# Two attention blocks on one core: tiles regrouped by heads, convolution taps shared out over three engines, horizontal offsets as differences, and minus the maximum in a row of q

## What is computed

```python
x = x + block0(_gn(x), ...)      # w_qkv, pooling taps, layer norms, rel_pos, w_proj
x = x + block1(_gn(x), ...)      # qkv_w with a low-rank addition to q and v, rel_pos, proj_w

# block0, for 12 heads of 16 channels
q, k, v = split(x @ w_qkv.T + b_qkv)
q = layer_norm(dwconv3x3(q, w_pool_q), g_q, b_q)      # likewise k and v, own taps, gains and biases
attn = einsum(q * scale, k) + rel_h[..., :, None] + rel_w[..., None, :]
o = softmax(attn) @ v + q                              # q is added again (ori_q)
y = o @ w_proj.T + b_proj
```

## Time and profile before

| what | us |
|---|---|
| median of 3 runs | 109.63 (109.55 to 111.31) |
| the profiled execution | 108.68 |
| its span, first to last instruction | 106.7 |

### The profile page before, as it was taken

One profiled execution on the slowest core, in us unless ns is written; L12 is line 12 of the kernel. 1 busy time (PEld: TensorE's weight loads), 2 busy tenths in 40 slices (PEclk: granted clock), 3 DMA queues, 4 the chain that ended last, 5 costly groups with the idle time before them and its releaser, 6 DMA issues.

```text
span 106.7 us, 2097 instructions
## 1 busy us (share of the span) xinstructions
PE 97.1 (91%) x822; PEld 70.8 (66%) x825; DVE 62.7 (59%) x134; ACT 51.3 (48%) x115; POOL 31.4 (29%) x46
## 2 busy tenths in 40 slices
PE   5799999999959999999999999899989999999780
PEld 2155787578848986777856563797759879857440
DVE  3469995587999667834650135464796493560130
ACT  4011904663534981837815624254246668715820
POOL 8947600599999999000000000000000000000000
PEclk9995579999999999999999999999999999999999
DMA  2999980000000000000000000000000000000002
GB/s 59 308 307 292 237 79 0 3 0 6 0 0 0 9 0 0 0 0 6 0 0 0 0 6 0 0 0 0 0 0 6 0 0 6 0 0 0 0 0 74
DMA packets 2826, 3.73 MB, mean 35 GB/s; under 512 B 305, under 2 KB 2242, under 8 KB 2818
## 3 DMA queue, kind: packets, MB, share of 16 engines
q0 software_dynamic: 784, 0.79, 6.7%
q1 hardware_dynamic: 1282, 1.41, 4.8%
q10 hardware_dynamic: 752, 1.42, 4.5%
HBM read 3.42 MB, written 0.20 MB: 34 GB/s over the span
## 4 chain that ended last, share of the span: by engine, by line
PE 75%; DVE 10%; ACT 7%; DMA 3%; issue 2%
PE bank L917 9%; PE bank L760 8%; PE bank L853 6%; PE bank L850 6%; PE bank L749 6%; PE bank L892 5%; PE bank L905 5%; PE bank L866 5%; PE bank L893 4%; PE bank L831 3%; ACT pt L386 3%; DVE taps_m L622 3%; DMA x<-x_t 3%; PE bank L734 3%; PE bank L832 2%
## 5 line engine op out<-in xcount | busy, mean ns | idle before, releaser
L575 DVE TENSOR_REDUCE mx<-bank 128x2 fp32r<-128x512 f32 x24 | 15.0, 682 | 3.2 <-PE bank L866 3.2
L386 ACT ACTIVATE pt<-bank 128x512 f32<-128x512 f32 x24 | 13.0, 594 | 3.6 <-PE bank L893 3.4
L892 PE MATMUL bank<-qs,ks 128*128 128x256 f32 x48 | 13.3, 310 | 0.8 <-ACT pt L386 0.7
L570 DVE SCALAR_TENSOR_TENSOR qs<-qs,vec,bank 64x512 fp32r<-64x512 f32 x12 | 8.8, 737 | 6.9 <-ACT qs L376 6.8
L893 PE MATMUL bank<-mt,nhot_r 128*128 128x256 f32 x48 | 12.0, 280 | 0.0
L892 PEld LDWEIGHTS bank<-qs,ks 128*128 128x128 f32 x48 | 9.0, 187 | 2.8 <-ACT pt L386 1.8
L760 PE MATMUL bank<-pad,taps_m 128*128 128x256 f32 x36 | 10.5, 445 | 0.2 <-DVE taps_m L622 0.2
L734 PE MATMUL bank<-warm 128*128 128x512 bf16 x28 | 9.0, 443 | 1.5 <-POOL warm L279 1.3
L324 POOL TENSOR_SCALAR tap_p<-pad,vec 64x256 f32<-64x256 f32 (+1 forms) x11 | 10.3, 937 | 0.0
L749 PE MATMUL bank<-xn,w 96*128 96x256 f32 (+1 forms) x40 | 9.6, 428 | 0.6 <-DVE xn L549 0.6
L376 ACT ACTIVATE qs<-bank 64x512 fp32r<-64x512 f32 x12 | 7.1, 590 | 6.2 <-PE bank L853 6.2
(11 more groups left out here) (103 smaller groups left out, 166.7 us busy)
## 6 DMA issues: line engine op xcount, KB each, us to landing
ks<-hots POOLq DMA_DIRECT2D x1, 768.0 KB, 7.8
wp<-w_proj ACTq DMA_DIRECT2D x1, 576.0 KB, 8.1
w<-w_qkv SPq DMA_DIRECT2D x1, 432.0 KB, 8.8
w<-w_qkv SPq DMA_DIRECT2D x1, 288.0 KB, 4.8
cst<-consts ACTq DMA_DIRECT2D x1, 256.0 KB, 4.8
nhot<-neg_hot ACTq DMA_DIRECT2D x1, 256.0 KB, 5.7
x<-x_t SPq DMA_DIRECT2D x1, 192.0 KB, 3.3
wpq<-w_proj_q ACTq DMA_DIRECT2D x1, 192.0 KB, 8.9
```

Of the source, the lines that this page charges most:

```text
L386: act.activation(pt[:, h, :, :], key_banks[h % 2][:, :].rearrange("p (k n) -> p k n", k=QT), ACT.Exp).then_inc(exped[b], 1)
L575: dve.tensor_reduce(mx[:, h, :], ring_bank(h // 4, 4 + h % 4)[:, :].rearrange("p (q n) -> p q n", q=QT), AXX, ALU.max).then_inc(maxed[b], 1)
L892: pe.matmul(dst, ks[:, h, k * 128:(k + 1) * 128], qs[:, h, :], start=True, stop=False)
```

## The change

- The q and k of one head group now share a tile: T0, T1, T2 hold q and k of heads 0 to 3, 4 to 7, 8 to 11 (weights' columns are reordered on the host); C and E hold v as before. A stage needs only its own tile. Both blocks use it; `late_k` goes.
- The taps are shared out: T0 three on PE and six on DVE, T1 five and four, C five on DVE and four on GpSimd, T2 six and three, E nine on GpSimd. Five tap matrices instead of eighteen are made, as T0 and T1 have the same taps: three by DVE, two by ACT. A centring pass adds the summed taps onto PE's.
- `normalise` multiplies gain and reciprocal deviation in one operation; the bias comes in ACT's high part, DVE's low part, `value` (DVE, for C and E) and `residual` (ACT, q rows for `q_project`).
- GpSimd makes the horizontal offsets as differences from the first key column's offset (`differences`), so that row 0 of `qs` is zero and free. `ks` row 0 is one everywhere (in `hots`, now laid out for 12 heads on the host), and minus the maximum is written into row 0 of `qs`: `turn_maxima` makes it as rows of one partition by eight matmuls with one column of weights (identity times -1), ACT copies two heads, DVE two. The matmuls with `nhot_r`, `nhot`'s transfer and `mt` go.
- x comes in two halves, on SP's and ACT's queues; warm-ups ahead of the group sums and behind them are 8 and 5 instead of 7 and 4, `lora_first` comes later, and two warm-ups in block 0's stage 1 go.
- `lora_second(0)` and `add_lora(0)` move from stage 1 to stage 2 of block 0, `q_project(0)` behind that stage.

```diff
+PE_TAPS = {T0: range(0, 3), T1: range(0, 5), C: (), T2: (), E: ()}
+DVE_TAPS = {T0: range(3, 9), T1: range(5, 9), C: range(0, 5), T2: range(0, 6)}
+POOL_TAPS = {C: range(5, 9), T2: range(6, 9), E: range(0, 9)}
+MATRICES = 5
...
-    sp.dma_start(xs[0][0:HALF], x_t.rearrange("(t p) n -> p t n", p=HALF)).then_inc(d_x, 16)
+    sp.dma_start(xs[0][0:HALF, 0], x_t[0:HALF]).then_inc(d_x[0], 16)
...
+    pool.wait_ge(d_rel, 16)
+    pool.wait_ge(d_vec, 16)
+    pool.wait_ge(rel_zeroed, 1)
+    def differences(b):
+        row = relt[64:128, 2 * b + 1, 0:1]
+        src = bass.AP(row.tensor, row.offset, [list(row.ap[0]), [1, SIDE], [1, SIDE]])
+        first = bass.AP(row.tensor, row.offset, [list(row.ap[0]), [1, SIDE], [0, SIDE]])
+        pool.tensor_tensor(dif[64:128, b], src, first, ALU.subtract).then_inc(dif_set, 1)
+        pool.wait_ge(dif_set, b + 1)
+        pool.tensor_copy(dif_hi[64:128, b], dif[64:128, b]).then_inc(dif_high, 1)
+        pool.wait_ge(dif_high, b + 1)
+        pool.tensor_scalar(dif_m[64:128, b], dif_hi[64:128, b].bitcast(F32), vec[64:128, MASK:MASK + 1], None,
+                           ALU.mult).then_inc(dif_masked, 1)
+        pool.wait_ge(dif_masked, b + 1)
+        for c in (0, 16):
+            pool.tensor_tensor(rel_w[64:128, 2 * b + 1, :, c:c + 16], dif_m[64:128, b], dif[64:128, b],
+                               ALU.add).then_inc(rel_set, 1)
+            pool.wait_ge(rel_set, 4 * b + c // 16 + 1)
+    def windows(b):
+        row = relt_s[64:128, 2 * b, 0:1]
+        src = bass.AP(row.tensor, row.offset, [list(row.ap[0]), [1, SIDE], [1, SIDE]])
+        for c in (32, 48):
+            pool.tensor_copy(rel_w[64:128, 2 * b, :, c:c + 16], src).then_inc(rel_set, 1)
+    differences(0)
     pool.wait_ge(rel_split, 1)
...
-    pool.wait_ge(p_sum, 2 * TAPS - D_SPLIT)
+    convolve_pool(C)
+    convolve_pool(T2)
+    pool.wait_ge(p_sum, pool_sums(T2))
+    pool.wait_ge(d_cst, 16)
+    ident_four = bass.AP(ident.tensor, ident.offset, [[ident.ap[0][0], HALF], [0, 4], [1, HALF]])
+    pool.tensor_copy(add_w[0:HALF].rearrange("p b t n -> p (b t) n"),
+                     ident_four).then_inc(add_set, 1)
+    pool.wait_ge(add_set, 1)
+    convolve_pool(E)
+    pool.wait_ge(p_sum, pool_sums(E))
+    differences(1)
...
+    act.dma_start(xs[0][0:HALF, 1], x_t[HALF:]).then_inc(d_x[1], 16)
...
-        if b == 0 and g == 0:
-            act.wait_ge(mt_zeroed, 1)
-        act.activation(mt[0:4, g, :], mt_ps, ACT.Copy).then_inc(max_c[b], 1)
+        act.wait_ge(max_t[b], 2 * g + 1)
+        act.activation(qs[0:1, 4 * g:4 * g + 2, :], mt_ps[0].rearrange("p (h n) -> p h n", h=2),
+                       ACT.Copy).then_inc(max_a[b], 1)
...
+        act.wait_ge(scaled, n_cen[t])
+        act.activation(hi[:, t, :], nrm[:, t, :], ACT.Identity,
+                       bias=vec[:, LNB0 + t:LNB0 + t + 1]).then_inc(hi_set[0], 1)
+    def residual(t):
+        to = qf[0:64, 0] if t == T0 else qf[64:128, 0] if t == T1 else qf[0:64, 1]
+        act.wait_ge(scaled, n_cen[t])
+        act.activation(to, nrm[0:64, t, :], ACT.Identity, bias=vec[0:64, LNB0 + t:LNB0 + t + 1]).then_inc(qf_set, 1)
...
     act.wait_ge(zeroed, 1)
-    pad_tile(0)
-    pad_tile(1)
+    pad_tile(T0)
+    pad_tile(C)
+    pad_tile(T1)
+    set_picks()
+    tile_stats(T0)
+    tap_matrices(PE_TAPS[T0].stop)
+    tile_rstd(T0)
+    pad_tile(T2)
+    high(T0)
     copy_lora()
...
-    tile_stats(B)
-    pad_tile(4)
-    high(A)
-    tile_rstd(B)
-    stage(0, 0, {0: lambda: high(B), 1: lambda: tile_stats(C), 2: lambda: tile_rstd(C), 3: lambda: tile_stats(D)})
-    stage(0, 1, {0: lambda: tile_rstd(D), 1: lambda: high(D)})
+    def k_stats():
+        tile_rstd(T1)
+    def after_first():
+        high(T1)
+        residual(T0)
+        pad_tile(E)
+    def c_in():
+        tile_stats(C)
+        tile_rstd(C)
+    stage(0, 0, {0: lambda: tile_stats(T1), 4: k_stats, 1: after_first, 3: c_in})
+    stage(0, 1, {0: lambda: residual(T1), 1: lambda: tile_stats(T2), 2: lambda: tile_rstd(T2), 3: lambda: high(T2)})
     stage(0, 2, {1: stats_e, 2: lambda: tile_rstd(E), 3: v_to_tokens_e})
+    residual(T2)
     last_stage(0)
...
+        dve.scalar_tensor_tensor(out=nrm[0:r, t, :], in0=cen_e[:] if t == E else cen_ps[t][0:r],
+                                 scalar=vec[0:r, LNG0 + t:LNG0 + t + 1], in1=rstd[0:r, t, :],
+                                 op0=ALU.mult, op1=ALU.mult).then_inc(scaled, 1)
+    def value(t):
+        r = ROWS[t]
+        dve.wait_ge(scaled, n_cen[t])
+        dve.tensor_scalar(full[0:r, (C, E).index(t), :], nrm[0:r, t, :], vec[0:r, LNB0 + t:LNB0 + t + 1], None,
+                          ALU.add).then_inc(full_set, 1)
...
+    def copy_maxima(b, g):
+        dve.wait_ge(max_t[b], 2 * g + 2)
+        dve.tensor_copy(qs[0:1, 4 * g + 2:4 * g + 4, :],
+                        mt_ps[1].rearrange("p (h n) -> p h n", h=2)).then_inc(max_d[b], 1)
...
+    taps(T0, 0, 6)
...
         dve.tensor_copy(va[:, :, 0:8, 0:HD],
                         turn_ps[:, 0:QT * HD * 8].rearrange("p (q h c) -> p q h c", q=QT, c=HD)).then_inc(v_set[0], 1)
-    def low_d_and_v():
-        low(D)
+    def t1_norm():
+        normalise(T1)
+    def t1_low():
+        low(T1)
+        taps(C, 3, 5)
+    def c_norm():
+        normalise(C)
+        value(C)
+    def t2_in():
         v_to_tokens()
-        add_lora(0)
-    stage(0, 0, {0: k_in, 2: lambda: taps(D, 2, 4), 3: lambda: taps(D, 4, D_SPLIT)})
-    normalise(C)
-    stage(0, 1, {1: lambda: normalise(D), 2: low_d_and_v})
-    stage(0, 2, {1: lambda: add_lora(1), 2: lambda: normalise(E)})
+        low(T2)
+    stage(0, 0, {1: lambda: taps(C, 1, 3), 4: t1_norm, 2: t1_low})
+    taps(T2, 0, 3)
+    c_norm()
+    stage(0, 1, {0: lambda: taps(T2, 3, 5), 1: lambda: taps(T2, 5, 6), 2: lambda: normalise(T2), 3: t2_in})
+    add_lora(0)
+    stage(0, 2, {1: lambda: add_lora(1), 2: lambda: (normalise(E), value(E))})
+    copy_maxima(0, HG - 1)
     o_norm(0, HG - 2)
     o_norm(0, HG - 1)
...
+    def convolve(t, first, last):
+        for k in PE_TAPS[t][first:last]:
+            if k == 0:
+                pe.wait_ge(padded, n_padded[t])
+            if t == T0:
+                pe.wait_ge(taps_d, k + 1)
+            if t == T1 and k == PE_TAPS[T0].stop:
+                pe.wait_ge(taps_a, MATRICES - PE_TAPS[T0].stop)
+            pe.matmul(cen_ps[t], taps_m[:, k, :], pad[:, t, k // 3:k // 3 + SIDE, k % 3:k % 3 + SIDE],
+                      start=(k == 0), stop=False, skip_group_check=True)
...
+    def centre_tile(t):
         r = ROWS[t]
-        if first == 0:
-            pe.wait_ge(qtaps_set if v == 0 else vtaps_set, TAPS)
-            pe.wait_ge(padded, order0.index(t) + 1)
-        for k in range(first, last):
-            mm = pe.matmul(cen_ps[t][0:r, :], taps_m[:, v, k, 0:r],
-                           pad[:, t, k // 3:k // 3 + SIDE, k % 3:k % 3 + SIDE],
-                           start=(k == 0), stop=(k == TAPS - 1))
-            if k == TAPS - 1:
-                mm.then_inc(centred, 1)
+        parts = []
+        if t in DVE_TAPS:
+            pe.wait_ge(conv_step[t], len(DVE_TAPS[t]))
+            parts.append(conv[0:r, conv_slot[t], :])
+        if t in POOL_TAPS:
+            pe.wait_ge(p_sum, pool_sums(t))
+            parts.append(conv_p[0:r, pool_order.index(t), :])
+        if t == T2:
+            pe.wait_ge(lora_c, 1)
+        if t == E:
...
-            dst = ring_bank(g, n)[:, j * TOK:(j + 1) * TOK]
-            pe.matmul(dst, pick[:, v, i:i + 2, :], hi[:, place3[t], :], start=True, stop=False)
-            mm = pe.matmul(dst, pick[:, v + 1, i:i + 2, :], lo[:, place3[t], :], start=False, stop=True)
+        for part, ready in enumerate((hi_set, lo_set)):
+            pe.wait_ge(ready[b], g + 1)
+            for j in range(2):
+                t, i = place(4 * g + 2 * j)
+                mm = pe.matmul(ring_bank(g, n)[:, j * TOK:(j + 1) * TOK], pick[:, v + part, i:i + 2, :],
+                               (hi, lo)[part][:, t, :], start=(part == 0 and j == 0), stop=(part == 1), skip_group_check=True)
...
         if g >= 1:
-            pe.wait_ge(exped[b], 4 * g - 1)
-        for q in range(QT):
-            mm = pe.matmul(mt_ps[:, q * 128:(q + 1) * 128], mx[:, 4 * g:4 * g + 4, q], ident_r[:],
-                           start=True, stop=True)
-        mm.then_inc(max_t[b], 1)
+            pe.wait_ge(exped[b], 4 * g)
+        for j in range(4):
+            for q in range(QT):
+                to = (j % 2) * TOK + q * 128
+                mm = pe.matmul(mt_ps[j // 2][:, to:to + 128], mx[:, 4 * g + j, q:q + 1], ident_r[:],
...
+                mm.then_inc(max_t[b], 1)
     def score_by_key(b, h):
         g, j = h // 4, h % 4
         if j == 0:
-            pe.wait_ge(max_c[b], g + 1)
-        if b == 0 and h == 1:
-            pe.wait_ge(logged, n_cen[D])
+            pe.wait_ge(max_a[b], g + 1)
+        if j == 1:
+            pe.wait_ge(max_d[b], g + 1)
         if h >= 2:
```

(37 more changed lines are left out.)

397 lines of the change are left out of this document (180 added, 217 removed).

## The result

The changed kernel took 116.17 us (median; 114.71 to 117.59) beside 109.59 us (109.41 to 111.31) for the kernel before on the same chip: a ratio of 1.0478, 95% interval 1.0447 to 1.0508. It is slower by 4.8%, where 108.3 us, a gain of 1.2%, was forecast; the range ended at 111.3. Its profiled execution took 114.81 us, the span of it 113.0 us, against 106.7 before.

The account below looks back on a forecast made before the run. PE work, busy 91%, was taken as the bound, with a DVE queue behind block 0's first scores. Block 0's 0.6 us and block 1's 0.7 made 1.3 us: 108.68 to 107.4 profiled, 108.3 median; range 105.5 to 111.3.

Parts of the forecast that it names:

- block 1's further 0.7: Block 1's gain of 0.7 us up to its direct sums, on top of block 0's 0.6.
- The 48 matmuls: Adding minus the maximum: 5.8 us of PE time, but only about 0.5 us a stage, 0.6 to 0.7 in a last stage.
- The head: Kernel start: 0.3 us from x in halves, T0 centred at 14.7 to 14.9, first pick at 18.7.
- the clock comes back sooner, or does not fall: Rival: the head's low clock from 8.0 ends early or never comes; 106.2 us taken, chance 0.25.
- the windows: Two GpSimd operations in the head, 0.9 us, following the differences; done at 13.5, wanted at 20.6, off the path.
- The turning: Maxima turned by eight one-column matmuls: 0.48 us, bounds 0.27 and 0.96, so +0.36 a stage.
- The copies: Copies of the turned maxima, one row of 512: ACT 0.37 to 0.59 us, DVE 0.41 to 0.69, upper ends taken.
- the gap: Block 0's stage 1: PE waits for DVE from 28.7 to 32.3, with only 0.5 us to do.
- the clock falls in the gap of stage 1: Rival: half clock in block 0 from the gap to 38 adds 3.0 us, giving 111.3; chance 0.20.
- the slower case: The rival "the clock falls in the gap of stage 1": 111.3 us, slower by 1.5%, chance 0.20.

Follow-up runs that it names:

- experiment 5: Changed kernel plus twelve zero matmuls in block 0's stage 1 gap and 512-column zero matmuls in PE's waits for exponentials: 111.69 us, ratio 1.0264.
- experiment 8: experiment 5 with the residual of T2 moved early on ScalarE, to the start of block 0's stage 2: 110.75 us.
- experiment 10: experiment 8 with the q projection put back in block 0's stage 2: 110.11 us.
- experiment 19: experiment 13 measured again in five rounds: 108.14 us, ratio 0.9841.
- experiment 9: Changed kernel with the maxima as before (two turning matmuls, 48 one-hot matmuls), so the tiles alone: 116.49 us, ratio 1.0703.
- experiment 6: Changed kernel with a zero matmul ahead of each of the 48 key-score matmuls and twelve in block 0's stage 1: 115.19 us.
- experiment 3: Kernel before without only the 48 matmuls that add minus the maximum: 115.44 us, beside 108.13 for the kernel before.
- experiment 12: Changed kernel with the maxima as before, twelve zero matmuls in stage 1's gap, residual of T2 early, q projection back in stage 2: 117.47 us.
- experiment 13: experiment 10 with lora_second(0) moved from stage 2's picks into PE's wait ahead of the first weighing: 106.75 us, ratio 0.9765.
- experiment 2: Changed kernel with twelve 256-column zero matmuls in block 0's stage 1, between the second pick and the turning: 112.33 us.
- experiment 1: Changed kernel with a 256-column zero matmul ahead of each of the 48 key-score matmuls: 117.73 us.
- experiment 11: Kernel before with 8 and 5 warm-ups in its head and x in two halves: 110.63 us, ratio 0.9988.
- experiment 14: experiment 7 measured again in more runs: 108.91 us, ratio 0.9896.
- experiment 20: Changed kernel with only lora_second(0), T2's residual and the q projection moved, no zero matmuls: 109.37 us, ratio 1.001.
- experiment 7: Kernel before with 8 and 5 warm-ups in its head instead of 7 and 4: 107.17 us, ratio 0.9861.

## Why the prediction was wrong

**The sum of the work was priced well, in part by luck.** Without its low time the changed kernel's S0 is 40.6 - 13.7 x 0.43 = 34.7 us; the forecast had 59.6 - 24.7 = 34.9. S1 is 41.8 - 6.8 x 0.43 = 38.9; the forecast, with block 1's further 0.7, had 38.9 too, and experiments 5, 8, 10 and 19 show 38.9 to 39.0 with no low clock at all. In S0 the agreement hides two misses: a wait of 1.0 us that the forecast overlooked (below), and 1.2 us by which the rest came out cheaper. The 48 matmuls are worth 0.6 to 0.7 us in block 1, as forecast (39.6 with them or with zero matmuls in their place and no low clock, experiments 9 and 6, 38.9 to 39.0 without), and not the 2.9 that half of 5.8 us of PE time seems to promise.

**The head was better than forecast.** T0's centring matmul ran at 12.86, not 14.7 to 14.9: the clock didn't fall at 8 (rival "the clock comes back sooner, or does not fall"), PE waited for DVE's taps, as that rival said. Two of those taps took 0.84 us each (at 11.11 and 11.98), beside GpSimd's two-tensor additions, where 0.58 a step was taken. Pick at 17.49 (18.7), scores at 24.05 (24.7), stage 1's relative unit at 30.77 (32.3).

GpSimd in order of time, where the differences meet DVE's taps:

```profile
8.58 0.61 POOL L306 TENSOR_TENSOR dif<-relt 64x256 f32<-64x256 f32 x1
9.25 0.39 POOL L308 CAST dif_hi<-dif 64x256 fp32r<-64x256 f32 x1
9.75 0.98 POOL L310 TENSOR_SCALAR dif_m<-dif_hi,vec 64x256 f32<-64x256 f32 x1
10.81 1.71 POOL L314 TENSOR_TENSOR rel_w<-dif_m,dif 64x256 fp32r<-64x256 f32 x2
13.58 1.06 POOL L323 CAST rel_w<-relt_s 64x256 fp32r<-64x256 f32 x2 [1.05 <-DVE relt_s L702]
```

The differences ended at 12.52 and the windows at 14.64, a microsecond later than the 13.5 forecast, since the windows waited 1.05 for DVE's split of the table; wanted at 19.59, they are on no path. The Trainium skill (GPSIMD Engine Reference, Specifications) names DVE operations with two SBUF inputs as those that contend; the trace agrees, and the price depends on what GpSimd runs: 0.60 (at 9.96) beside its one-tensor mask, 0.84 beside its two-tensor additions.

**The small new operations.** The turning took 0.48 for eight, as taken, between its bounds of 0.27 and 0.96. The copies are at their upper ends (groups by form, columns as in the earlier trace rows):

```profile
L637 DVE CAST qs<-bank 1x512 fp32r<-1x512 f32 x6 | 4.1, 677 | 7.7 <-PE bank L948 7.6
L408 ACT ACTIVATE qs<-bank 1x512 fp32r<-1x512 f32 x6 | 3.5, 584 | 4.0 <-PE bank L948 3.9
```

DVE was the releaser of PE's wait in the gap, 1.50 us ahead of the turning, as forecast.

**The step that failed is the clock behind the first scores.** The forecast put it at full level there in both blocks, so the low clock was a term of nothing in its sum, and only the rival "the clock falls in the gap of stage 1" gave it a price: one fall, +3.0 us, with a chance of 0.20. Measured were four falls, two in each block, 20.5 us low and some 8.8 us of time. The rival's mechanism ran: the clock fell at 32.5, behind the gap, with +3.0 forecast for it and 7.0 us low x 0.43 = 3.0 measured. Against it stood that the old kernel idled 1.2 of 3.8 us and kept the clock. That argument took the busy share of a stretch for what the clock follows. It isn't: 2.67 of 3.40 busy was followed by a fall here, 2.62 of 3.80 before wasn't, and 3.35 of 3.40 was followed by one at 87.25. What the prediction never asked is what else the 48 matmuls did. They are the dense part of each output side (128 rows by 128 columns, 256 wide), and between them stand relative units, turnings and low-rank matmuls, small and many. Experiment 3 takes only them from the old kernel and loses 4.1 us by the fastest runs, 7.3 by the medians; experiments 5 and 9 put dense work back in two ways and block 1 has no fall, while in experiment 12 it has one.

The second term missed is the move of `lora_second(0)` beside stage 2's picks, the new turning and a relative unit. It was priced as 0.82 us of PE time. Between experiments 10 and 13 its place is the only difference, and in the profiled executions stage 2's fall went with it: 6.8 us low in the changed kernel and 10.2 in experiment 10, 2.9 to 4.4 us of time. It is not the only way to that fall: in experiment 3 it stands in stage 1 and stage 2 falls all the same. The Trainium skill (TensorE: Matmul & The Clock Gate, The HAM clock gate) has the throttled state as the default that activity has to release. That sentence stood in the prediction as speaking for the slower case, and the runs side with it over the single row that stood against it. It gives no reason for the falls behind 3.35 and 3.40 of 3.40 us busy.

**The sum.** Forecast span 106.7 - 1.3 = 105.4. Add 8.8 for the low clock; take off 0.65 for the head up to the scores, 0.2 for S0's working and 0.4 for the tail (6.6 us behind block 1's direct sums against 6.95): 112.95, of 113.0 measured. The price of 0.43 is known to some 0.02, so this sum holds to half a microsecond at best. Of S0, 1.0 us is a wait that the forecast overlooked: `q_project(0)`, moved behind stage 2, waits for ScalarE's residual of T2, which was queued behind the output copy.

One row of PE in order of time:

```profile
58.30 1.03 PE L987 MATMUL bank<-qf,wpq 128*96 128x256 f32 x3 [1.00 <-ACT qf L500]
```

**What stays open.** Which property of a stretch of matmuls the clock follows: columns of weights, rows, width or distance all differ at once between the dense and the thin ones. No run separates them. It is open, too, why the clock of the same kernel falls behind the gap of stage 1 in one execution (19) and not in another (13); the head differed by 0.3 us. And the fall in experiment 2, behind 3.40 of 3.40 us busy, is tied by experiment 13 to what stands in that place, since without `lora_second(0)` it went; whether its matmuls of 16 rows hold the clock less, or only their 0.8 us at that moment, isn't shown.

## What to carry to other kernels

Before you take matmuls out of a kernel, ask what they do for the clock: dense matmuls between small ones can cost little and hold it up, and where other engines pace the stage anyway, taking them away gains little (0.7 us a block here) and may cost several times that. Look at the clock line first after a change and price each low microsecond (0.43 us here); a busy share near 90% is no protection. Put small, unhurried matmuls into PE's waits rather than beside other small ones. Where times vary between executions of one kernel, compare segments behind the head, and look at the mean clock of every execution before you call one profile the rule.

## What the runs showed of the hardware

**The clock record begins late.** The profile gives 1.00 until its first recorded change. The warm-ups at the start say otherwise. Of the changed kernel and of experiment 13, PE in order of time:

```profile
0.98 3.60 PE L804 MATMUL bank<-warm 128*128 128x512 bf16 x8 [0.98 <-POOL warm L285]
```

```profile
5.68 2.29 PE L803 MATMUL bank<-warm 128*128 128x512 bf16 x5
```

Five such matmuls take 1.24 us in the changed kernel's block 1, at full clock:

```profile
68.31 1.24 PE L804 MATMUL bank<-warm 128*128 128x512 bf16 x5
```

Eight in 3.60 us are 0.45 each, against 0.25, near the pace of 1.2 GHz. The five behind the group sums took 1.24 us in the changed kernel's execution and 2.29 in experiment 13's, though both records read 1.00.

**The start differs from execution to execution.** Experiments 1, 6, 10 to 14, 19 and 20 show 2.29 us for these five, the changed kernel and experiments 2, 5, 7, 8 and 9 1.24. In the new order the first scores lie at 24.9 to 25.6 us where these five take 2.29 us and at 23.9 to 24.1 where they take 1.24 (27.75 in experiment 9, with its dip); in the old order with 8 and 5 warm-ups at 26.69 (7) and 30.64 (14, with a dip too). Within one series the times of a kernel spread by 2.5 to 7.6 us, later falls included, those of the kernel before from 107.7 to 112.9 over all later series. The Trainium skill (TensorE: Matmul & The Clock Gate, The HAM clock gate) says that the number of slow matmuls at a start varies between runs of one kernel; the rows agree. Two more warm-ups don't remove the old kernel's low clock reliably either (experiment 7): the profiled execution of experiment 14 had a dip from 27.25 to 30.5.

**Less work can take longer.** Without 48 of its matmuls PE was busy for 104.7 us instead of 97.1 (experiment 3).
